# A batch's first block turn moved into the batch before it, the output weights asked for later, and vector work reordered around routing

## The reference, cut to what matters

```python
q = x @ wq; k = x @ wk; v = x @ wv        # x: 8 batches, 512 tokens, 512 wide; 16 query heads, 4 key/value heads of 128
o = softmax(mask(q @ k.T / sqrt(128))) @ v # each key/value head serves 4 query heads; causal
x1 = layernorm(x + o @ wo)
logits = clip(x1 @ gate_w.T, -50, 50)      # 8 experts
top_w, top_idx = top_k(logits, 2); rw = softmax(top_w)
deltas = softmax(expert_atom_weights) @ atoms
weighted = deltas * sigmoid(importance)    # 4096 entries for each expert
vals = einsum(rw, weighted[top_idx])
out = layernorm(x1 + x1 @ W.T + segment_sum(x1[:, cols] * vals, rows))
```

## Time and profile before

| | us |
|---|---|
| median of 3 runs | 1853.06 |
| runs | 1845.52 to 1854.03 |
| profiled execution | 1849.14 |
| its span, first to last instruction | 1847.3 |
| TensorE matmul busy | 1732.2 (94%) |
| VectorE busy | 1297.7 (70%) |
| ScalarE busy | 810.6 (44%) |
| GpSimd busy | 843.3 (46%) |

### The profile page before, as it was taken

One profiled execution on the slowest core, in us unless ns is written; L12 is line 12 of the kernel. 1 busy time (PEld: TensorE's weight loads), 2 busy tenths in 40 slices (PEclk: granted clock), 3 DMA queues, 4 the chain that ended last, 5 costly groups with the idle time before them and its releaser, 6 DMA issues.

```text
span 1847.3 us, 33274 instructions
## 1 busy us (share of the span) xinstructions
PE 1732.2 (94%) x8750; PEld 1450.6 (79%) x8750; DVE 1297.7 (70%) x4027; ACT 810.6 (44%) x1950; POOL 843.3 (46%) x1221
## 2 busy tenths in 40 slices
PE   8999999998999899999999999989998999989983
PEld 7888878887888788877887788878887778777772
DVE  5566568866887688768886788678867876662356
ACT  4444344434443444534553445444543443333454
POOL 6775355534554244333334333343333333665564
PEclk9999999999999999999999999999999999999997
DMA  9655455655555766666665676566666558444698
GB/s 327 233 213 197 171 186 186 185 163 200 172 173 166 236 206 205 200 218 207 229 217 180 187 226 230 196 191 231 209 208 224 175 168 326 144 149 143 225 334 329
DMA packets 195148, 386.41 MB, mean 209 GB/s; under 512 B 27328, under 2 KB 98144, under 8 KB 184480
## 3 DMA queue, kind: packets, MB, share of 16 engines
q1 hardware_dynamic: 176688, 344.53, 54.9%
q0 software_dynamic: 18288, 39.80, 6.8%
HBM read 261.64 MB, written 122.62 MB: 208 GB/s over the span
## 4 chain that ended last, share of the span: by engine, by line
PE 66%; DVE 13%; issue 9%; DMA 5%; ACT 3%; POOL 2%; SPq 1%; DVEq 1%; another core or an unknown queue 0%; ACTq 0%; POOLq 0%
PE psum L1607 19%; PE psum L1609 18%; PE psum L1608 18%; PE psum L1635 4%; PE psum L2488 2%; PE psum L2490 2%; PE psum L2489 2%; DVE pT_lo L2064 2%; DMA probs_strips<-probs_blocks 1%; DVE probs_blocks L2076 1%; DVE route_product L700 1%; DVE probs L2053 1%; DMA probs_moved<-probs_strips 1%; DMA token_rows<-x,ids_now 1%; PE psum L376 1%
## 5 line engine op out<-in xcount | busy, mean ns | idle before, releaser
L1471 POOL TENSOR_SCALAR probs<-probs,row_inv 128x128 f32<-128x128 f32 (+3 forms) x512 | 295.4, 602 | 432.3 <-DVE row_inv L2061 431.1
L1913 ACT ACTIVATE probs<-probs,neg_max 128x512 f32<-128x512 f32 (+3 forms) x512 | 281.7, 553 | 192.4 <-DVE neg_max L2053 191.8
L1607 PE MATMUL psum<-xT_hi,w_hi 128*128 128x512 f32 x640 | 256.8, 401 | 16.3 <-DVE oT_lo L2064 16.0
L1609 PE MATMUL psum<-xT_hi,w_lo 128*128 128x512 f32 x640 | 251.5, 393 | 0.0
L1608 PE MATMUL psum<-xT_lo,w_hi 128*128 128x512 f32 x640 | 250.9, 392 | 0.0
L1935 ACT ACTIVATE qT_hi<-psum 128x512 fp32r<-128x512 f32 x128 | 76.7, 600 | 388.1 <-PE psum L1609 383.7
L2053 DVE CUSTOM_DVE_ANT_0 probs<-psum,causal 128x512 f32<-128x512 f32 (+3 forms) x512 | 220.8, 485 | 27.7 <-issue 16.0
L1607 PE MATMUL psum<-wo_hi,oT_hi 128*128 128x512 f32 x496 | 199.2, 402 | 16.4 <-DVE y_acc L2111 9.4
L1609 PE MATMUL psum<-wo_hi,oT_lo 128*128 128x512 f32 x496 | 194.2, 392 | 0.0
L1608 PE MATMUL psum<-wo_lo,oT_hi 128*128 128x512 f32 x496 | 193.9, 391 | 0.0
L1607 PE MATMUL psum<-kT_hi,qT_hi 128*128 128x512 f32 (+3 forms) x512 | 166.4, 325 | 1.5 <-DVE qT_lo L2097 1.3
(11 more groups left out here) (255 smaller groups left out, 4101.5 us busy)
## 6 DMA issues: line engine op xcount, KB each, us to landing
w_hi<-split_qk_weights SPq DMA_DIRECT2D x140, 256.0 KB, 5.7
w_lo<-split_qk_weights SPq DMA_DIRECT2D x140, 256.0 KB, 6.8
probs_strips<-probs_blocks SPq DMA_DIRECT2D x54, 640.0 KB
probs_moved<-probs_strips SPq DMA_DIRECT2D x216, 160.0 KB
wo_hi<-split_out_weights SPq DMA_DIRECT2D x27, 1024.0 KB
wo_lo<-split_out_weights SPq DMA_DIRECT2D x27, 1024.0 KB
expert_weights_hi_lo<-split_expert_weights SPq DMA_DIRECT2D x8, 2048.0 KB, 9.5
x_in<-in_L_attn_x_dram SPq DMA_DIRECT2D x8, 1024.0 KB, 6.0
```

Of the source, the lines that this page charges most:

```text
L1471: last = pool.tensor_scalar(p, p, row_inv[:, buf, i:i + 1], 1.0, ALU.mult, ALU.mult)
L1607: pe.matmul(dst, hi_s, hi_m, start=start, stop=False)
L1609: return pe.matmul(dst, lo_s, hi_m, start=False, stop=stop)
L1913: last = act.activation(probs[:, buf, a:a + w], probs[:, buf, a:a + w], ACT.Exp, bias=neg_max[:, buf, i:i + 1], scale=-1.0, accum_out=row_ ...
```

## The change

On SyncE, `move(it, 0)` leaves the "first" group and is issued as `move(it + 1, 0)` in the "batch" group before it, ahead of the residual store. `fetch_wo` of a "first" group goes from before slot 3 to behind `move(it, 1)`. On VectorE, `turn_blocks` of that head goes along, between `ranked` and `add_rows(it, 2)`. In a moved "first" group, `kT` and `inverse(n + 3)` and `oT(n, 0, 0)` now have two logits ahead of them where there were six, and `route_best` goes behind `qT(n + 4)`. In moved "group" and "batch" groups, `route_variance` goes behind `maxima(n + 2, 0)` and `route_normalize` behind `pT(n, 1)`; in a "group", logit 5 goes behind `oT(n, 0, 0)`. No arithmetic is added or taken away.

```diff
--- before.py
+++ after.py
@@ -1348,7 +1348,7 @@
         def iteration(b, g, it, kind, route, job):
             n = it * G
             after, second = (g + 1) % HKV, (g + 2) % HKV
-            if is_moved(kind, route):
+            if is_moved(kind, route) and kind != "first":
                 move(it, 0, 3 * n)
             if route and kind == "first":
 
@@ -1360,8 +1360,6 @@
                 if g == 0:
                     sp.wait_ge(s_scatter, 16 * (NJ + 1))
                 load_piece(b, g)
-            if route and kind == "first":
-                fetch_wo(it, g)
             slot(3, it + 1, after)
             if not route and g < len(PART_PAIRS):
                 store_pair(PART_PAIRS[g][0])
@@ -1382,13 +1380,13 @@
                 keep_wo(it)
             if is_moved(kind, route):
                 move(it, 1, 3 * (n + 2) + 3)
+            if route and kind != "end":
+                fetch_wo(it, g)
             if route and kind == "first" and not past_end(it + HKV):
 
                 wait_apart(sp, s_seed, b + 1, s_passed)
                 wait_apart(sp, s_xt, (b + 1) * C, s_passed)
                 sp.dma_start(x_in[:], x_rows[bass.ds(b + 1, 1)].rearrange("a p t d -> (a p) t d")).then_inc(s_x_in, 16)
-            if route and kind not in ("first", "end"):
-                fetch_wo(it, g)
             for j in range(3):
                 slot(j, it + 2, second)
             if not route and g < len(PART_PAIRS):
@@ -1430,6 +1428,7 @@
 
                 sp.wait_ge(s_wo_kept, 32 * RAW)
             if kind == "batch":
+                move(it + 1, 0, 3 * (n + G))
 
                 wait_apart(sp, s_y_acc, TT + (it + 1) * TT, s_passed)
                 sp.dma_start(r_store[bass.ds(b, 1)].rearrange("a p t d -> (a p) t d"), y_acc[:]).then_inc(s_r_out, 16)
@@ -2148,25 +2147,26 @@
                 route_places(dve, R, tt - 1)
             if moved:
                 qT(n + 2, 0, BANK_A)
-                turn_blocks(n, it, 0)
+                if kind != "first":
+                    turn_blocks(n, it, 0)
                 inverse(n + 1, 1)
             if not route and kind == "first":
                 split_entries(dve, N)
             if not route and g:
                 keep_sums(dve, N, psum, BANKS_PT[0], g - 1, entry_sum)
-            if early:
+            if early and not moved:
                 route_variance(dve, R, tt)
             if kind != "first":
                 add_rows(it - 1, 1, "group")
             if moved:
                 dve.wait_ge(s_blocks, moved_number(it, 0) + 1)
                 maxima(n + 2, 0)
+                if early:
+                    route_variance(dve, R, tt)
             else:
                 inverse(n + 1, 1)
                 qT(n + 2, 0, BANK_A)
                 pT(n, 0, moved)
-            if early and kind != "end":
-                route_normalize(dve, R, tt)
             if kind == "end":
                 route_normalize(dve, R, tt)
             if early and not moved:
@@ -2179,6 +2179,7 @@
                 qT(n + 3, 1, BANK_A)
             pT(n, 1, moved)
             if early and moved:
+                route_normalize(dve, R, tt)
                 route_logits(dve, R, tt, (0,), products)
             if late and not moved:
                 route_variance(dve, R, tt)
@@ -2229,23 +2230,25 @@
                 route_logits(dve, R, tt, (2,) if kind == "batch" else (3,), products)
             if late and moved:
                 route_normalize(dve, R, tt)
-                route_logits(dve, R, tt, (0, 1, 2), products)
-            if route and kind != "batch":
-                route_logits(dve, R, tt, (4,) if early else (3,), products)
+                route_logits(dve, R, tt, (0,), products)
+                kT(it + 1)
+                route_logits(dve, R, tt, (1,), products)
+            if early and kind != "batch":
+                route_logits(dve, R, tt, (4,), products)
             for q in quads[1:2]:
                 equal_indices(dve, N, q)
             inverse(n + 3, 1)
-            if route and kind != "batch":
-                route_logits(dve, R, tt, (5,) if early else (4, 5), products)
+            if kind == "end":
+                route_logits(dve, R, tt, (5,), products)
             for q in quads[1:2]:
                 count_later(dve, N, upper, q)
-            if key_first:
+            if key_first and not late:
                 kT(it + 1)
             oT(n, 0, 0, banks)
             if kind == "end":
                 pT(n, 2, moved)
             if route:
-                route_logits(dve, R, tt, (3,) if kind == "batch" else (6,), products)
+                route_logits(dve, R, tt, {"first": (2,), "group": (5,), "batch": (3,), "end": (6,)}[kind], products)
             for q in quads[2:3]:
                 equal_indices(dve, N, q)
             if kind == "end":
@@ -2257,17 +2260,19 @@
                 route_logits(dve, R, tt, (4, 5), products)
                 kT(it + 1)
             if route:
-                route_logits(dve, R, tt, (6, 7) if kind == "batch" else (7,), products)
+                route_logits(dve, R, tt, {"first": range(3, NE), "group": (6, 7), "batch": (6, 7), "end": (7,)}[kind], products)
             for q in quads[2:3]:
                 count_later(dve, N, upper, q)
             if not key_first and kind != "end" and not route:
                 kT(it + 1)
             if kind != "end" and not moved:
                 pT(n, 2, moved)
-            if route:
+            if route and not late:
                 route_best(dve, R, tt)
             if kind != "end":
                 qT(n + 4, 0, bank_of_query(0, banks))
+            if late:
+                route_best(dve, R, tt)
             if route:
                 route_chosen(dve, R, tt)
             if kind != "end":
@@ -2319,6 +2324,8 @@
                 if route:
                     route_shares(dve, R, tt)
                     ranked()
+                if kind == "batch":
+                    turn_blocks(n + G, it + 1, 0)
                 add_rows(it, 2, kind)
                 if route:
                     route_places(dve, R, tt)
```

## The result

The changed kernel takes **1858.8 us** in the median (1853.1 to 1864.6, 20 runs) where the kernel before takes 1848.5 beside it (1841.5 to 1856.0, 20 runs). The ratio is **1.0052**, 95% interval 1.004 to 1.0064: some 9.6 us slower, where 0.25% faster was forecast. The profiled execution of after spans 1860.4 us against 1847.3, at a mean granted clock of 0.979 against 0.985.

A forecast was written before the change was run, and what follows sets the result against it. Matmuls on TensorE hold 94% of the span, so only its idle stretches and clock count. Terms -1.2 + 4.8 - 2.5 - 2.4 - 3.1 = -4.4 us gave 1844.7 from the profile, 1848.7 from the median; predicted 1848.5, range 1836 to 1858.

The forecast's parts named there:

- The border's two waits: TensorE's waits B and C in "first" groups: sum unchanged in batches 1 to 6, gain 1.2 us in batch 7.
- B: TensorE's wait for oT_lo ahead of query 0 in a "first" group, 1.54 us; said to fall to nothing.
- C: TensorE's wait for pT_lo ahead of values_second in a "first" group, 1.97 us; said to become 3.5 us.
- Rival 1: Border gain kept because the freed queue lands second strips sooner: -18.4 us, 1834.7; chance 0.15.
- The clock: Half clock on TensorE expected behind C in all seven batches: loss 4.8 us, bounds 0 and 6.8.
- Loss 1.7 + 2 x 0.7 + 1.7 = 4.8: New half clock behind C in batches 1, 3, 6 and 7, partly absorbed in batches 3 to 6.
- A: TensorE's wait for GpSimd's low part of v in a "first" group, 1.18 us; said to stay.
- The moved blocks: turn_blocks and strips moved into the batch before: 0 us; without slack 0.6 x 7 = 4.2.
- so this costs nothing: VectorE's first maxima, pushed back about 0.6 us, are taken by ScalarE some 3 us later: 0 us.
- Later groups: Moving route_variance and others cuts waits ahead of out_rows(2): gains 2.5, 2.4 (split batches) and 3.1 us (batch 7).
- In batches 1 and 2 TensorE waits nowhere else: In later groups of batches 1 and 2, the saved y_acc waits are kept: gain 6 x 0.41 = 2.5 us.
- Output weights: Asked for behind the moved strips, said to arrive before out_rows(0): 0 us, bounds 0 and 12.

The follow-up runs named there:

- g3: Store edit alone on the kernel before: in "first" groups the store of the routed rows goes behind the second strips; 1834.0 against 1850.8 us, ratio 0.9901.
- e6: The changed kernel with the store of the routed rows behind the second strips in "first" groups; 1822.4 against 1835.5 us, ratio 0.9925 to the kernel before.
- e7: The changed kernel without the moved blocks and strips, with the store of the routed rows behind the second strips in "first" groups; 1816.9 us, ratio 0.9906.
- e2: The kernel before with only VectorE's new order in the border ("first") group; 1844.8 against 1836.0 us, ratio 1.0049.
- e1: The kernel before with only the border head's block turn and strips moved into the batch before; 1841.8 against 1836.0 us, ratio 1.0031.
- e5: The changed kernel with the border head's block turn and strips put back into the "first" group; 1841.1 against 1835.5 us, ratio 1.0031 to the kernel before.
- e8: The kernel before plus three unread VectorE transposes in the last group of each routed batch, nothing moved; 1841.4 against 1835.5 us, ratio 1.0043.
- e3: The kernel before with only the later groups' edits (variance, normalize and logit 5 moved back); 1833.6 us, ratio 0.9991.
- g2: e7 with a "first" group's output weights asked for early again, where the kernel before asks for them; 1837.6 against 1850.8 us, ratio 0.9909.
- e4: The kernel before with only the output weights asked for behind the second strips in a border group; 1838.8 us, ratio 1.0019.
- g4: The kernel before with the "first" groups' new VectorE order and the store of the routed rows behind the second strips; 1836.5 us, ratio 0.992.
- g1: e7 with route_normalize ahead of pT(n, 1), not behind it, in later groups with routing; 1831.9 against 1850.8 us, ratio 0.9895.

## Why the prediction was wrong, step by step

- **The border's two waits: right.** B near 0, C 3.3 to 4.05 where 3.5 was said, since `route_store` holds the strips; the 1.2 us of batch 7 came out as 17.13 - 15.94 = 1.2. That `route_store` alone sets the transfer is shown by g3, e6 and e7. Rival 1 was rightly set aside, and its size (-18.4 us) is about what the store edit gives, which does free the strips: a ratio of 0.9901 is 18 us.
- **The clock: right in kind, too small.** The step that failed is "Loss 1.7 + 2 x 0.7 + 1.7 = 4.8". Half clock did stand behind every C, but the seven batches pay 8.5 us more up to `out_rows(0)`, above even the bound of 6.8. (The half clock behind B of batch 7, now gone, lies ahead of `values_second` and is already in that batch's 1.2.) Batches 1 and 7 pay 1.3 and 1.7, near what was said; batches 3 and 6 pay 2.1 and 2.5 where 0.7 was said, and batch 5 pays 0.9 where nothing was. I gave each stretch 3.4 us, and in these three batches it was 6.8. I also let the waits ahead of `out_rows(2)` absorb a part, in the same sum in which the later groups' edits remove these waits. e2 shows the term by itself. It costs 8.8 us (5.9 to 12.1), though from A to `values_second` its seven batches take 111.8 us in all against 112.5. They take 7.6 us more up to `out_rows(0)` and 8.2 more up to `out_rows(2)` of the next group, so in all nothing is absorbed even where those waits are left.
- **The moved blocks: the step "so this costs nothing" failed too.** e1 gives +5.8 us, and e5 beside the whole change some 4 (0 to 8). I had read the border at the head of batch 3, where a loop is left, VectorE idles and a later start is absorbed. At the heads of batches 2, 4, 5 and 6 a loop turns back; there VectorE has its stop of about 3 us, little or nothing absorbs the moved 1.8 us, and `qT_lo`, which TensorE needs first, comes out later. The same instructions, at the old place, had followed behind `qT_lo`. I priced the missing slack at 0.6 x 7; in the changed kernel the wait grew by 1.3 to 1.8 us in four batches and by nothing in three. e8 shows that VectorE's time alone makes such waits.
- **Later groups: -8.0 forecast, -1.7 measured (e3, -3.7 to +0.4).** "In batches 1 and 2 TensorE waits nowhere else" was true of the kernel before and no ground for keeping the gain: VectorE was only just in time for `oT_lo`, so 0.42 us given at `y_acc` came back as 0.59 and 0.79 at query 0 and as 0.74 and 0.48 for `pT_lo` in the last groups. Where 2.5 us were to be gained, these two batches lose 1.0 and 0.9 us. In the split batches the return was foreseen and was nearly complete: 1.59 us in e3 where 1.37 and 0.50 stood before. The cost of normalize at its new place, 1.42 for 0.54 us, was missed.
- **Output weights: 0 forecast.** No wait at `out_rows(0)` came, as said. g2 beside e7 shows no cost, within intervals that would hide one of 3 us; e4 says about 3 us. Open.

The border groups changed by -0.8 us up to `values_second` (batch 7's -1.2, and +0.4 in the other six) and by +8.5 behind it. With e5's or e1's size for the blocks and e3's for the later groups the sum is -0.8 + 8.5 + 4 (or 5.8) - 1.7 = +10.0 (or 11.8), against 9.6 (7.4 to 11.8) measured. It mixes single traces with runs and leaves out e4's open 3 us, so it fits only roughly. The prediction's own slow prices, taken together, would have said this much: -1.2 + 6.8 for the clock + 4.2 for the blocks + 0 for the later groups = +9.8. But each unknown was let end near its favourable side, and no rival put the slow prices together. The range was also called wide enough for "nearly all of" rival 1, whose own time, 1834.7, lies outside it.

## What to carry to other kernels

Before freeing an engine ahead of a wait, find who holds the transfer that ends the next wait: here one store, queued on SyncE ahead of strips that leave 9 us before it once they are free (615.25 and 624.11 in g3), was worth 1% by itself, and all the reordering of VectorE on top of it nothing that could be measured. Two short waits joined into one long wait are not neutral, since here every joined wait of 3.26 us or more had half clock behind it. Slack must be read at every kind of border a line of code runs at: here the turn of a loop had little or none, where the same lines had plenty when the loop was left.

## What the runs showed of the hardware that was not expected

- **VectorE's stop at a loop's turn.** 2.5 to 4.3 us of idle with nothing to wait for in the profile (before: 2.57, 3.28, 4.25, 3.58 at the heads of batches 2, 4, 5, 6; after: 2.61, 3.20, 3.14, 3.14), ahead of the first instruction of the loop's body. It isn't of a fixed length: at batches 4, 5 and 6 it was 2.5 to 2.6 in e8, where VectorE came late, and 4.2 to 4.3 in g3 and e5, and what sets it isn't shown. Two 8 KB transfers of an instruction queue lie in or right behind it, at 802.2 and 804.6 us in after and at 792.9 and 796.4 in the kernel before; whose they are isn't shown. The Trainium skill's page "Runtime: NRT & Kernel Launch", section "Instruction fetch mechanics", says that a taken branch to a place outside the fetched pages forces a fetch before execution can go on. The rows agree with it in that the stop stands where a loop turns and not where it is left; that it is such a fetch isn't shown.
- **The length of half clock.** Behind gathered waits of 3.26 to 4.50 us there was half clock 21 times in 21 (after, e2, e5), for 3.4 us in some batches and 6.8 in others, and in batch 3 of after it began at 645.3, inside the wait and 2.2 us ahead of its end. Shorter waits give no sure answer. Behind 1.51 to 1.63 us in batches 2 to 6 of g3 and e7 there was none, but behind 1.63 in batch 2 of e3 and 1.65 in batch 1 of e7 there was. Behind 1.90 and 1.89 in g4 there was, but not behind 2.42 in batch 6 of e4 or 2.78 in batch 7 of e7. So a trace of another execution may show it at other places. The Trainium skill's page "TensorE: Matmul & The Clock Gate", section "HAM oscillation — how this bites in real kernels", describes stretches of matmuls that each start at half rate behind a wait for data; the changed kernel does this seven times in seven, as e2 does.
- **An instruction that gets longer by its neighbour.** Normalize takes 0.54 or 0.55 us in the 20 "group" and "batch" groups of the kernel before, and 1.41 to 1.47 us in the same groups of batches 1 and 2 of e3, always while GpSimd scales `probs` (284.32 to 288.16); in the other batches, with GpSimd beside it for 0.45 us, it takes 0.72. In "first" groups it takes 1.30 to 1.37 even in the kernel before, each time beside GpSimd's low part of v. In g1, ahead of GpSimd's work, it is 0.52, and it stays 0.52 in batches 3 to 7, where GpSimd's scaling starts 0.23 us before it ends. The Trainium skill's page "SBUF — State Buffer", section "Who interferes with whom", says that VectorE's `tensor_scalar` can share a port pair with GpSimd, which whoever comes first holds for its whole instruction; the traces agree that it gets much longer only where GpSimd's work was under way first.
